# One quarter of each odd adjacency tile, and layer 0's own rows, each loaded by two transfers instead of one, in a two-layer graph attention kernel

## What is computed

```
layer 0: h = x @ W; e = leaky_relu(h @ a1 [:,None] + h @ a2 [None,:], 0.2)
         out = elu(softmax(where(adj > 0, e, -9e15)) @ h)
layer 1: q, k, v = x @ Wq.T + bq, x @ Wk.T + bk, x @ Wv.T + bv
         out = elu(softmax(where(adj > 0, q @ k.T / sqrt(128), -9e15)) @ v)
```

## Time and profile before

| | us |
|---|---|
| median of three runs | 1697.23 |
| the profiled execution, its own time | 1699.37 |
| its span, first to last instruction | 1697.6 |
| TensorE busy / VectorE busy / GpSimd busy / ScalarE busy | 1189.3 / 1201.7 / 1137.3 / 904.9 |
| adjacency loads, 256 of 1024 KB, median from issue to landing | 22.4 |
| own rows for layer 0, 64 of 66 KB, median from issue to landing | 17.5 |

### The profile page before, as it was taken

How to read it: one execution, slowest core, us unless ns; L and a number is a source line. 1 busy time by engine, 2 the same in 40 slices (tenths; PEclk the granted TensorE clock), 3 DMA queues, 4 the chain that set the end, 5 groups by cost and what they waited for, 6 DMA issues and landing times.

```text
span 1697.6 us, 23065 instructions
## 1 busy us (share of the span) xinstructions
PE 1189.3 (70%) x5362; PEld 930.2 (55%) x5362; DVE 1201.7 (71%) x6497; ACT 904.9 (53%) x1827; POOL 1137.3 (67%) x1206
## 2 busy tenths in 40 slices
PE   2667777777777777777765467776777677676665
PEld 1344545545545554544455466766666566666664
DVE  3567988888888888888887366656655665566655
ACT  2769877877878778887852222333233323332322
POOL 1227777766766666666666477777777777777773
PEclk9778777777777777777765555556665666666755
DMA  9869999999999999999942122222222222222221
GB/s 292 345 225 391 397 398 399 400 401 396 390 386 394 365 371 390 382 394 371 386 125 61 51 59 57 65 64 66 64 66 64 66 64 64 66 64 64 66 66 39
DMA packets 122263, 372.41 MB, mean 219 GB/s; under 512 B 34577, under 2 KB 67858, under 8 KB 89362
## 3 DMA queue, kind: packets, MB, share of 16 engines
q1 hardware_dynamic: 75458, 289.83, 44.3%
q0 software_dynamic: 38464, 81.08, 17.1%
q10 hardware_dynamic: 8208, 0.03, 0.3%
HBM read 358.12 MB, written 12.72 MB: 218 GB/s over the span
## 4 chain that ended last, share of the span: by engine, by line
DMA 40%; POOL 33%; issue 13%; ACT 5%; DVE 4%; PE 3%; SPq 2%; POOLq 0%; ACTq 0%; DVEq 0%
DMA arena<-in_adj_dram 37%; POOL arena L601 32%; ACT arena L1166 4%; DMA table<-arena 1%; POOL arena L571 1%; SPq L444 1%; DMA arena<-table 1%; DVE arena L658 1%; SPq L447 1%; PE psum L1368 0%; DVE arena L866 0%; PE psum L1429 0%; DMA arena<-table,arena 0%; PE psum L1393 0%; PE psum L1415 0%
## 5 line engine op out<-in xcount | busy, mean ns | idle before, releaser
L571 POOL DMA_INDIRECT arena<-table,arena x576 | 558.7, 970 | 252.5 <-issue 164.6
L601 POOL DMA_INDIRECT arena<-table,arena x576 | 550.3, 955 | 184.0 <-issue 174.9
L1166 ACT ACTIVATE arena<-arena 128x2048 bf16<-128x2048 int32 x256 | 487.9, 1906 | 163.3 <-DMA arena<-in_adj_dram 160.7
L1368 PE MATMUL psum<-arena 128*128 128x512 bf16 x1024 | 301.6, 437 | 71.7 <-ACT arena L1166 71.3
L866 DVE SCALAR_TENSOR_TENSOR arena<-arena 128x131 f32<-128x131 f32 (+1 forms) x768 | 267.3, 348 | 15.2
L1415 PE MATMUL psum<-arena 128*128 128x131 f32 (+1 forms) x768 | 200.7, 433 | 104.1 <-ACT arena L1303 102.4
L1401 PE MATMUL psum<-arena 128*128 128x18 f32 x768 | 144.6, 321 | 143.7 <-DVE arena L830 143.2
L1415 PEld LDWEIGHTS psum<-arena 128*128 128x128 f32 x768 | 179.9, 330 | 107.7 <-issue 107.7
L1368 PEld LDWEIGHTS psum<-arena 128*128 128x128 bf16 x1024 | 111.3, 118 | 221.2 <-ACT arena L1166 90.7
L1401 PEld LDWEIGHTS psum<-arena 128*128 128x128 f32 x768 | 138.5, 265 | 161.9 <-DVE arena L830 161.8
L1112 DVE CUSTOM_DVE_ANT_0 arena<-arena,psum 128x129 f32<-128x129 f32 x192 | 45.2, 286 | 226.4 <-DMA arena<-table,arena 226.4
(11 more groups left out here) (197 smaller groups left out, 1951.7 us busy)
## 6 DMA issues: line engine op xcount, KB each, us to landing
arena<-in_adj_dram SPq DMA_DIRECT2D x256, 1024.0 KB, 22.4
arena<-table,arena POOLq DMA_INDIRECT x1152
table<-arena POOLq DMA_DIRECT2D x32, 132.0 KB, 4.5
arena<-table SPq DMA_DIRECT2D x64, 66.0 KB, 17.5
table<-arena SPq DMA_DIRECT2D x16, 256.0 KB
arena<-table SPq DMA_DIRECT2D x64, 64.0 KB, 1.9
out_dram<-arena SPq DMA_DIRECT2D x16, 256.0 KB, 2.4
arena<-in_x_dram SPq DMA_DIRECT2D x4, 0.5 KB, 12.1
```

The lines of the kernel that those rows point to most:

```text
L571: pool.indirect_dma_start(Gt[:, v % GROUP, c + 1, :], None, table0, bass.IndirectOffsetOnAxis(idx_now[:, v % GROUP, c:c + 1], 0))\
L601: pool.indirect_dma_start(Gt[:, t % GROUP, c + 1, 0:D], None, table1, bass.IndirectOffsetOnAxis(idx_now[:, t % GROUP, c:c + 1], 0))\
L1166: nc.scalar.activation(mask[:, k, q * QUARTER:(q + 1) * QUARTER], adj_sb[:, k, q, :], ACT.Relu, accum_out=sum_all[:, bass.ds(tile, 1), q:q ...
L1368: nc.tensor.matmul(V[k], shifted[:, s, :], mask[:, k, s * 512:(s + 1) * 512], start=(s == 0), stop=False)
```

## The change

It declares five semaphores and cuts two kinds of loads in two. The first quarter of every tile that goes into buffer 1 (the odd tiles) is loaded as rows 0 to 119 on the old semaphore and rows 120 to 127 on `adj_rest_in`, and ACT waits for both. The other seven quarter loads in eight stay whole. The own rows of layer 0 are loaded as rows 0 to 103 and rows 104 to 127, for all tiles, and VectorE waits for both parts. The same bytes go to the same places.

```diff
+        adj_rest_in = sem("adj_rest_in")
+        self_rest_in = [sem(f"self_rest_in{k}") for k in range(GROUP)]
...
+        WIDE = 120
+        SELF_WIDE = 104
...
             def load_adj(tile, k, q):
+                if k == 1 and q == 0:
+                    sp.dma_start(adj_sb[0:WIDE, k, q, :], adj[bass.ds(tile * P, WIDE), 0:QUARTER]).then_inc(adj_in[k][q], 16)
+                    sp.dma_start(adj_sb[WIDE:P, k, q, :], adj[bass.ds(tile * P + WIDE, P - WIDE), 0:QUARTER])\
+                      .then_inc(adj_rest_in, 16)
+                    return
                 sp.dma_start(adj_sb[:, k, q, :], adj[bass.ds(tile * P, P), q * QUARTER:(q + 1) * QUARTER])\
                   .then_inc(adj_in[k][q], 16)
...
             def load_self(v, k):
-                sp.dma_start(Gt[:, k, 0, :], table0[bass.ds(v * P + 1, P), :]).then_inc(self_in[k], 16)
+                sp.dma_start(Gt[0:SELF_WIDE, k, 0, :], table0[bass.ds(v * P + 1, SELF_WIDE), :]).then_inc(self_in[k], 16)
+                sp.dma_start(Gt[SELF_WIDE:P, k, 0, :], table0[bass.ds(v * P + 1 + SELF_WIDE, P - SELF_WIDE), :])\
+                  .then_inc(self_rest_in[k], 16)
...
             def score0(u, k, r, n):
                 dve.wait_ge(rows_in[r], 16 * (ROWS - 1) * n)
                 dve.wait_ge(self_in[r], 16 * n)
+                dve.wait_ge(self_rest_in[r], 16 * n)
...
             def read_quarter(tile, k, q, nth):
                 act.wait_ge(adj_in[k][q], 16 * nth)
+                if k == 1 and q == 0:
+                    act.wait_ge(adj_rest_in, 16 * nth)
```

## The result

The changed kernel takes 1876.6 us, median of four runs (1870.75 to 1880.96), against 1697.6 us for the kernel before in the same comparison: a ratio of 1.106 (95% interval 1.1046 to 1.1075), 179 us slower. I had predicted 1685 us, and 1709 us at the slow end of the range.

The account below looks back on a forecast made before the run. The prediction took full DMA engines, with one late, to bound the adjacency loads. Sparing that engine, -23.3 us, and the others' added rows, +11.3 us, gave -12.0 us: 1685 us from a median of 1697.2, range 1674 to 1709.

Parts of the forecast that it names:

- What bounds the kernel now: Up to 860 us the DMA engines are full with adjacency loads; the change touches only this part, later work keeps its length.
- One engine seems to be last: In the adjacency loads one DMA engine is 4.7% behind fifteen others, perhaps because it carries the instruction fetches.
- Who carries which rows: 120, 8, 104 and 24 rows run on 15, 8, 13 and 12 engines; whole transfers use sixteen, eight rows each.
- If the late engine is the one that is spared: In the adjacency loads its load falls by 12%, it stops being last, and loads come at the others' pace: -23.3 us.
- Rival A: The late engine gets the ninth row of the adjacency loads instead of being spared: +11.7 us, 1709 us; chance 0.20.
- The price for the others: Eight engines carry 1.67% more bytes over the adjacency loads: +11.3 us at most, possibly nothing if they have slack.
- Rival C: The split adjacency load itself is slow, taking half as long again: +30 us, 1727 us; chance 0.05.
- SP's issues: Three more transfers per two tiles, 1.04 us, hidden behind SP's own waiting: 0 us, or 28 us without that cover.
- the waits added: ACT's second wait for the eight rows and VectorE's third for own rows: 0 us beyond the ninth row already counted.
- Own rows: Layer 0's own rows in two parts give eight engines 4 x 528 B more per two tiles, 0.34%.
- What would show it: Signs from 440 to 860 us: 390 GB/s or more if right, about 374 under rival A; ACT's adjacency wait falls from 86.6 us.

Follow-up runs that it names:

- the probe: The kernel before with eight small loads of 1 to 15 rows of 32 bytes added per four tiles, behind the adjacency loads: 1699.5 us, ratio 1.0021.
- the stretches: Two kernels that change how odd tiles' first quarter is loaded every ten to sixteen tiles: 1794.4 us against 1695.5 and 1779.2 against 1698.1 for the kernel before.

## Why the prediction was wrong

- *What bounds the kernel now*: right. Everything lay in the adjacency loads, and the second layer kept its 724 us.
- *One engine seems to be last*: right. The completions show one engine 9.6 us behind fifteen in the kernel before, and the probe's run again. That the instruction fetches make it late was not tested.
- *Who carries which rows*: right to the packet (800).
- *If the late engine is the one that is spared*: this step failed first. The late engine was not spared: it is the last to complete in every 120-row, 8-row, 104-row and 24-row load of the changed kernel, and so got the ninth row. The -23.3 us never came. Rival A had that right, with a chance of 0.20. The trace of before could have told that one engine is late, but not which. The Trainium skill's statement that I weighed, that engines 7 and 15 are usually slower (DMA: Bandwidth & Descriptors, Latency and other measured facts), does not agree with the records here: one engine alone is late in the whole loads, and it is among the four of the 4-row probe, by that numbering engines 0 to 3.
- *The price for the others*: this is the step that cost the range. I sized it by bytes, 1.67% and 11.3 us for all, and wrote that above "it is this". Bytes were not the price: 112 and 16 rows, with the bytes of each engine unchanged, cost 4.1 us a turn. The split load of 120 and 8 rows costs 5.6 us a turn in the kernel with the adjacency part alone (31.55 against 25.95, 167 us in all) and 6.4 to 6.6 in the stretches, and what the experiments leave as its cause is which rows each engine writes. Of the turn's gain, 5.6 us is the late engine's later landing (22.7 to 28.3); the fifteen, for whom I had set this price, land as before.
- *Rival C* named the mechanism, "engines may get in each other's way at the memory", with 0.05 and a price of half a load, 1.55 us a turn. It was 5.6 to 6.6 us, twice the split load's own 3.1 us. I had bounded it by the load itself, as if only its own packets could suffer. Packets of whole loads suffer too: one packet in six is long where one in eight is of a split load, and not the 120-row loads alone land late, as C's sign had it, but the whole ones with them (28.6 and 28.3 us). And the loop is closed: SP issues only when ACT has read, so what the late engine loses the others lose as well. In the changed kernel, four stretches of 4 us show it as an alternation, not as one rate:

```profile
597.00:601.00 4.00, 3.90 (x15) 3.28 (x16) 3.93 (x22) 1.87 (x3) 3.09 (x4) 0.50 0.92 323
601.00:605.00 4.00, 3.71 (x16) 1.79 (x15) 3.55 (x22) 4.00 (x7) 1.55 (x2) 0.78 0.55 127
...
609.00:613.00 4.00, 2.79 (x14) 2.69 (x14) 3.38 (x15) 1.39 (x5) 3.07 (x4) 0.57 0.62 112
...
617.00:621.00 4.00, 1.49 (x9) 0.68 (x8) 3.54 (x19) 3.73 (x7) 0.39 (x1) 0.85 1.06 304
```

  From 609 to 613 us the engines are busy for 62% of the time and move 112 GB/s; from 617 to 621 us all are full (1.06) at three quarters of the rate before. Over the whole stretch from 440 to 860 us the longer packets (390 ns for 329, a fifth) make most of the loss of rate, and the fall of the share from 1.00 to 0.95 the rest. Why it is the late engine that falls further behind isn't settled: no packet's record names its engine.
- *SP's issues, the waits added*: right at zero. The probe adds 128 small issues and waits while adjacency is loaded (152 in all) for 3.7 us, and the cut by columns costs nothing.
- *Own rows*: priced at 0.34%, 2.3 us, measured 16.1 us. The 8192-byte packets hardly lengthen there (1.9% are long). The late engine takes part in both pieces. Whether its added rows cost so much, or the small packets meet, no run tells.
- *What would show it*: the GB/s of the stretch, 390 or more if right, about 374 under A, was 308. ACT's wait for adjacency rose to 149.5 us where I had it fall. Those signs did their work.

## What to carry to other kernels

A transfer over all partitions is more than its bytes. Where such loads fill the DMA engines, every cut by rows that was tried, into equal shares (64 and 64, 112 and 16) or not, cost 4.1 to 6.6 us for one load of 3.1 us in eight, and it slowed the whole loads beside it. The same load cut by columns cost nothing: cut a load by columns if it has to be cut. Before work is moved off a late engine, find out which one it is. The completions of the ordinary loads show whether one is late at all, and a few 32-byte loads of 1, 2, 4, 8 and 15 rows in the stream show which sizes of load it takes part in, for 4 us.

## What the runs showed of the hardware that I had not expected

One load in eight, cut by rows, slows a saturated stream from 380 to 308 GB/s, while the engines' busy share falls only from 1.00 to 0.95. The busy share doesn't show the rate. And the same kernel takes 1695 to 1698 us on some chips and 2129 to 2145 us on others. On the second kind ACT idles up to 10 us at a time for nothing that the profile shows, the adjacency isn't waited for, and a change of 10% in the loads is invisible: an experiment there could have passed for proof that the split is free.
